# One FFN head's weights from two ScalarE passes, and its sums on VectorE in every other tile

## The chip, the cores and the metric

One core of a Trainium2 chip runs the program. The metric is the device time of one execution in microseconds (us), smaller being better; the median of three runs stands for the kernel.

## The reference

A pre-norm block over 16 sequences of 512 tokens with 128 channels: windowed attention with 16 heads, and then a feed-forward layer that picks its experts by product keys. Only the latter is touched by the change:

```python
xn = batchnorm(layernorm(x))                       # over all 8192 tokens
q = (xn @ w_q.T) -> 2 halves, 8 heads
sim = einsum(q, keys)                              # 32 similarities per half and head
sx, sy = top8(sim[0]), top8(sim[1])
scores, idx = top8 of the 64 sums sx[i] + sy[j]    # experts i * 32 + j, of 1024
o = gelu(x . key_in[idx]) * softmax(scores)
out = sum over heads and picked experts of o * key_out[idx]
```

## The kernel before

Attention runs first (to about 710 us) and is the same in both kernels. The FFN then works without a gather. For each tile of 128 tokens (64 tiles in 16 groups of 4, tile k = 0 to 3 of a group) and each of the 8 heads it makes a dense row of weights over all 1024 experts:

- GpSimd (`pair_sums`, L772) adds the 32 similarities of one half to the 32 of the other: SUM, 1024 elements per token, in a ring of 16 buffers, two tiles' worth. A buffer is free when the mask that reads it has run (`sum_buffer_free`).
- ScalarE (L873) makes E = exp(SUM + NB) into one of two PSUM buffers. NB = -log(sum) - maximum, so E is the softmax value. Exp h waits for the pair sum h and for mask h-2, whose E buffer it takes.
- VectorE (L965) makes W = (SUM >= the eighth best score) * E, the "mask". W has 8 buffers.
- TensorE (L1033) turns W with eight transposes per head and adds up the heads in PSUM (WT), in one buffer.
- After head 7 VectorE (`experts`, L948) multiplies WT by the Gelu values GE of all experts to CT, inside the next tile (h=1), and TensorE multiplies CT by key_out (`outputs`, L997 and L1000).

The order of each engine's work is written out by hand as a loop over the heads h of a tile. VectorE also does the ranking for the tiles ahead, in eight parts (`choose`): 0 to 3 are MAX8 over the similarities, 4 and 5 the candidates and the top 8 of each head (TOP), with D8 = scores less their maximum; 6 is the sum Z of their exps and 7 is NB. EVEN_PARTS and ODD_PARTS say ahead of which mask each part stands: in even tiles parts 0 to 5 of the next tile and 0, 1 of the one after stand ahead of mask 4, in odd tiles 2 and 3 ahead of masks 2 and 3, and 4, 5 ahead of mask 4; parts 6 and 7 ahead of masks 6 and 7 in both. ScalarE copies products out of PSUM between its exps (GE at h=1 and h=3, OUT at h=5, SIM at h=7), does a small exp and a logarithm for the next tile after exps 5 and 6, and in even tiles, behind exp 3, applies Gelu to half of a group's GE, between two table loads (L806, L807). M8X and TOP are in PSUM (SMALL), M8Y, CD, D8, Z, LZ, NB and SIM in SBUF.

L404 and L410 are two small operations of VectorE in attention. Both take two tensors of 32x128: L404 one from PSUM and one from SBUF, L410 (rm and mp) both from SBUF. GpSimd runs L261 in attention, the masking of the exps.

Of the kernel before, what the change touches and what calls it, by code (L numbers as in the profile page):

```python
# [33 lines left out]
P = 128  # L34
# [630 lines left out]
WRING = 8  # L665

EVEN_PARTS = ((), (), (), (), ((1, 0), (1, 1), (1, 2), (1, 3), (1, 4), (1, 5), (2, 0), (2, 1)), (), ((1, 6),), ((1, 7),))
# [7 lines left out]
def ffn(nc, ctx, x1, x2T, KM, key_in, key_out, gb, ident, bnst, first, out):  # L675
# [6 lines left out]
    def sem(name):  # L682
# [23 lines left out]
    NB = [sb(f"NB{b}", [P, FH]) for b in range(2)]  # L706
    SUM = [sb(f"SUM{b}", [P, NE]) for b in range(RING)]
# [6 lines left out]
    SMALL = ps("SMALL", [P, 4, FH, TOPK])  # L714
# [6 lines left out]
             "out_stored ranked candidates top_ready top_less_max top_exp exp_sum log_sum bias_ready").split()  # L721
# [46 lines left out]

    def pair_sums(eng, j, h, q):
# [4 lines left out]
    def sum_buffer_free(eng, j, h):  # L774

        wait_pos(eng, S["weights_masked"], j * FH + h - RING + 1)

    @block.gpsimd
    def _(pool):
# [5 lines left out]
        def group(g, b, more):  # L785
            for k in range(GT):
                j = g * GT + k
                pool.wait_ge(S["sim_copied"], j + 1)
                for h in range(FH):
                    sum_buffer_free(pool, j, h)  # L790
                    pair_sums(nc.gpsimd, j, h, k).then_inc(S["pair_sums"], 1)
# [4 lines left out]
    def _(act):  # L796
# [45 lines left out]

        small_exp(0)
        small_ln(0)

        def group(g, b, more):
            for k in range(GT):
# [4 lines left out]
                for h in range(FH):  # L852
# [18 lines left out]
                    act.wait_ge(S["pair_sums"], j * FH + h + 1)  # L871
                    wait_pos(act, S["weights_masked"], j * FH + h - 1)
                    nc.scalar.activation(E[h % 2][:, :], SUM[(k * FH + h) % RING][:, :], ACT.Exp, bias=NB[q][:, h:h + 1]).then_inc(S["exp_ready"], 1)  # L873

# [13 lines left out]
    def _(dve):  # L888
# [13 lines left out]
        def choose(part, j, r, q):  # L902
# [19 lines left out]
            if part == 5:  # L922
# [6 lines left out]
                nc.vector.tensor_tensor(D8[:, :, :], TOP[q][:, :, :], CD[:, :, 0:1].broadcast_to([P, FH, TOPK]), ALU.subtract).then_inc(S["top_less_max"], 1)  # L929
            if part == 6:  # L930
                dve.wait_ge(S["top_exp"], j + 1)
                nc.vector.tensor_reduce(Z[:, :], E8[:, :, :], AX.X, ALU.add).then_inc(S["exp_sum"], 1)
            if part == 7:
                dve.wait_ge(S["log_sum"], j + 1)

                nc.vector.scalar_tensor_tensor(out=NB[q][:, :], in0=LZ[:, :], scalar=-1.0, in1=TOP[q][:, :, 0], op0=ALU.mult, op1=ALU.subtract).then_inc(S["bias_ready"], 1)

# [12 lines left out]
        def group(g, b, more):  # L950
            for k in range(GT):
# [4 lines left out]
                for h in range(FH):  # L956
# [3 lines left out]
                    if h == 1 and real:  # L960
                        experts(*prev)

                    dve.wait_ge(S["exp_ready"], j * FH + h + 1)
                    wait_pos(dve, S["weights_turned"], j * FH + h - WRING + 1)
                    nc.vector.scalar_tensor_tensor(out=W[h % WRING][:, :], in0=SUM[(k * FH + h) % RING][:, :], scalar=TOP[q][:, h, TOPK - 1:TOPK],  # L965
                                                   in1=E[h % 2][:, :], op0=ALU.is_ge, op1=ALU.mult).then_inc(S["weights_masked"], 1)
# [5 lines left out]
    def _(pe):  # L972
# [30 lines left out]
        def group(g, b, more):  # L1003
            for k in range(GT):
                j = g * GT + k
                real = not (isinstance(j, int) and j == 0)
                for h in range(FH):
# [19 lines left out]
                    pe.wait_ge(S["weights_masked"], j * FH + h + 1)  # L1027
# [70 lines left out]
```

## Time and profile before

| | us |
|---|---|
| median of three runs | 1721.02 (1718.32 to 1722.32) |
| profiled execution | 1717.66, its span 1715.9 |
| busy: TensorE, VectorE, ScalarE, GpSimd | 1490.5, 1502.3, 1264.6, 1330.6 |
| GpSimd's pair sums, 512 of them | 958.5 |
| VectorE's masks, 512 | 641.9 |
| ScalarE's exps, 512 | 566.6 |
| TensorE's granted clock, mean | 0.956 of full speed |

The sums, masks and exps are all in the FFN, some 1000 us long. Four engines are busy for some 85 to 100% of it, so busy shares don't name the bound by themselves; the order of starts within a pair of tiles does, and the groups of rows below follow that order. A duration in the rows is that of one instruction as recorded; neighbours on one engine overlap by some 0.05 to 0.1 us, so the distance between two starts is a little less than the duration.

### The profile page before, as it was taken

The numbers are of one execution on the slowest core, as the hardware profiler recorded it, in microseconds if no ns is written. First come the engines' busy times: TensorE is split into PE (matmuls) and PEld (weight loads), VectorE is DVE, ScalarE is ACT, GpSimd is POOL, SyncE is SP. The second block draws the span as 40 slices with busy tenths as digits, with TensorE's granted clock in tenths as the row PEclk, the third lists the DMA queues.
The fourth block names the chain that finished last, engine by engine and source line by source line (L and its number), as shares of the span: only waits on it lengthen the run. The fifth ranks groups of instructions, "written<-read, shape, count | busy, mean of one in ns | idle before, by whom it ended". The sixth has DMA issues, their size and how long they took to land.

```text
span 1715.9 us, 33034 instructions
## 1 busy us (share of the span) xinstructions
PE 1490.5 (87%) x10688; PEld 1029.4 (60%) x10688; DVE 1502.3 (88%) x4488; ACT 1264.6 (74%) x1741; POOL 1330.6 (78%) x1579
## 2 busy tenths in 40 slices
PE   3799999999999998678888888888888888888877
PEld 2355555555555554367667666676666766667766
DVE  3889999999999985389999999999999999999998
ACT  1166666666666666378888888888888888888885
POOL 1055555556655556499999999999999999999993
PEclk9799999999999999789999999999999999999999
DMA  5344445444555440100000000000000000000000
GB/s 139 88 99 105 109 111 118 111 110 103 119 113 111 103 103 22 62 1 19 1 20 20 1 19 19 7 13 19 19 1 20 20 1 19 19 8 13 14 7 7
DMA packets 73627, 86.37 MB, mean 50 GB/s; under 512 B 9872, under 2 KB 63760, under 8 KB 68752
## 3 DMA queue, kind: packets, MB, share of 16 engines
q1 hardware_dynamic: 73456, 84.27, 20.7%
q8 instruction: 85, 1.39, 0.4%
q14 instruction: 86, 0.70, 0.2%
HBM read 58.30 MB, written 25.95 MB: 49 GB/s over the span
## 4 chain that ended last, share of the span: by engine, by line
POOL 47%; issue 5%; ACT 3%; DVE 2%; PE 1%; ACTq 0%; DVEq 0%; SPq 0%
POOL SUM L772 47%; ACT E L873 2%; DVE W L965 2%; ACT L807 1%; ACT GE L806 0%; PE WT L1033 0%; PE MB L1000 0%; PE E L988 0%; DVE CT L948 0%; DVE M8Y L909 0%; DVE SMALL L926 0%; ACT L806 0%; ACT SIM L800 0%; PE MB L975 0%; DVE SMALL L909 0%
## 5 line engine op out<-in xcount | busy, mean ns | idle before, releaser
L772 POOL TENSOR_TENSOR SUM<-SIM 128x1024 f32<-128x1024 f32 x512 | 958.5, 1928 | 11.5 <-DVE W L965 7.9
L965 DVE SCALAR_TENSOR_TENSOR W<-SUM,SMALL,E 128x1024 f32<-128x1024 f32 x512 | 641.9, 1279 | 46.4 <-ACT E L873 44.7
L873 ACT ACTIVATE E<-SUM,NB 128x1024 f32<-128x1024 f32 x512 | 566.6, 1118 | 102.1 <-DVE W L965 86.9
L1033 PEld LDWEIGHTS WT<-idf,W 128*128 128x128 f32 x4096 | 497.3, 151 | 231.3 <-DVE W L965 120.6
L1033 PE MATMUL WT<-idf,W 128*128 128x128 f32 x4096 | 570.8, 292 | 69.3 <-DVE CT L948 38.0
L261 POOL TENSOR_SCALAR_AFFINE_SELECT PT<-PT 128x128 f32<-128x128 f32 (+1 forms) x1024 | 336.9, 355 | 257.8 <-ACT PT L355 224.2
L414 DVE CUSTOM_DVE_ANT_0 SY<-SY,bandf 128x384 f32<-128x384 f32 x512 | 273.3, 574 | 0.0
L355 ACT ACTIVATE PT<-TX 128x512 f32<-128x512 f32 x256 | 153.0, 598 | 113.6 <-PE TX L542 113.4
L429 DVE TENSOR_REDUCE mx<-SX 128x2 f32<-128x512 f32 x256 | 174.5, 682 | 59.8 <-PE SX L524 59.7
L357 ACT ACTIVATE PT<-TY 128x768 f32<-128x768 f32 x256 | 207.4, 810 | 3.7
L570 PE MATMUL PV<-PT,V 128*32 128x384 f32 (+1 forms) x2048 | 165.5, 441 | 2.6 <-POOL PT L261 2.4
L516 PE MATMUL SY<-K,Q 72*128 72x384 bf16 x512 | 144.0, 339 | 8.4 <-DVE mx L414 4.3
L542 PE MATMUL TY<-Q,K 75*128 75x384 bf16 x512 | 125.9, 328 | 11.5 <-ACT PT L357 10.4
L975 PE MATMUL MB<-KM,BNT 128*128 128x512 f32 x128 | 72.1, 645 | 71.2 <-ACT OUT L820 69.4
L1000 PE MATMUL MB<-KO,CT 128*128 128x128 f32 x1024 | 124.9, 275 | 1.1 <-DVE CT L948 1.1
L516 PE MATMUL SX<-K,Q 72*128 72x256 bf16 x512 | 102.0, 281 | 24.4 <-DMA Q<-q_parts 18.9
L1000 PEld LDWEIGHTS MB<-KO,CT 128*128 128x128 f32 x1024 | 119.5, 192 | 1.3 <-DVE CT L948 1.3
L542 PE MATMUL TX<-Q,K 75*128 75x256 bf16 x512 | 99.6, 276 | 3.9 <-ACT PT L355 2.7
L948 DVE TENSOR_TENSOR CT<-WT,GE 128x1024 f32<-128x1024 f32 x64 | 78.4, 1225 | 20.2 <-PE WT L1033 20.2
L542 PEld LDWEIGHTS TX<-Q,K 75*128 75x128 bf16 x512 | 37.6, 98 | 97.2 <-issue 82.2
L570 PEld LDWEIGHTS PV<-PT,V 128*32 128x32 f32 x2048 | 53.6, 109 | 68.1 <-issue 47.9
L516 PEld LDWEIGHTS SX<-K,Q 72*128 72x128 bf16 x512 | 48.7, 100 | 67.3 <-issue 18.6
(110 smaller groups left out, 1638.9 us busy)
## 6 DMA issues: line engine op xcount, KB each, us to landing
K<-k_parts SPq DMA_DIRECT2D x96, 192.0 KB
Q<-q_parts SPq DMA_DIRECT2D x288, 64.0 KB
q_parts<-qp SPq DMA_DIRECT2D x16, 384.0 KB, 2.4
k_parts<-kp SPq DMA_DIRECT2D x16, 384.0 KB, 2.4
xin<-in_x SPq DMA_DIRECT2D x16, 256.0 KB, 3.1
xres<-in_x SPq DMA_DIRECT2D x16, 256.0 KB, 9.5
x<-X SPq DMA_DIRECT2D x16, 256.0 KB, 2.2
x2T<-X2T SPq DMA_DIRECT2D x16, 256.0 KB, 2.1
```

What stands on the lines that cost most here:

```text
L261: return nc.gpsimd.affine_select(out=out, in_=out, compare_op=ALU.is_ge, fill=0.0, base=0, pattern=([[0, 2]] if pairs else []) + [[s, P]], ...
L357: nc.scalar.activation(pt[:, 512:1280].rearrange("p (j n) -> p j n", j=2), TY[:, :, 0:384], ACT.Exp).then_inc(S["inner_exp"], 1)
L414: return nc.vector.tensor_tensor_reduce(out=scores, in0=scores, in1=bandf[:, k0 * P:k1 * P], scale=1.0, scalar=-3e38, op0=ALU.add, op1=ALU ...
L429: nc.vector.tensor_reduce(mx[:, h, 0:4:3], SX[:, :, :], AX.X, ALU.max).then_inc(S["outer_maxima"], 1)
L516: return pe.matmul(out, Q[b][0:KQ, h, i * P:(i + 1) * P], K[b][0:KQ, h, k0 * P:k1 * P], start=clear, stop=done, skip_group_check=True)
L542: return pe.matmul(out[:, 0:(q1 - q0) * P], K[b][0:R, h, j * P:(j + 1) * P], Q[b][0:R, h, q0 * P:q1 * P], start=True, stop=True, skip_grou ...
L570: o = pe.matmul(PV[32 * e:32 * e + 32, q0 * P:q1 * P], V[b][:, slot:slot + SLOT_V], PT[:, h % 8, at:at + (q1 - q0) * P], start=(j == 0 and ...
L772: return eng.tensor_tensor(SUM[(q * FH + h) % RING][:, :].rearrange("p (i j) -> p i j", i=NK), sx, sy, ALU.add)
L873: nc.scalar.activation(E[h % 2][:, :], SUM[(k * FH + h) % RING][:, :], ACT.Exp, bias=NB[q][:, h:h + 1]).then_inc(S["exp_ready"], 1)
L965: nc.vector.scalar_tensor_tensor(out=W[h % WRING][:, :], in0=SUM[(k * FH + h) % RING][:, :], scalar=TOP[q][:, h, TOPK - 1:TOPK], in1=E[h % ...
L1000: o = pe.matmul(po, CT[k % 2][:, e, :], key_out[:, e, :], start=False, stop=(e == BLK - 1))
L1033: o = pe.matmul(WT[:, e, :], W[h % WRING][:, e * P:(e + 1) * P], ident[:, :], is_transpose=True, start=(h == 0 and e % 4 == 0), stop=(h == ...
```

## The change

Head 3 (LH) gets its weights in another way, and in odd tiles its pair sum comes from another engine.

- ScalarE: ahead of exp 2 it applies Prelu in place to head 3's SUM with bias NT = -(eighth best score) and a slope of 1e30 for negative values (`l_shift`). A selected sum keeps its distance to the eighth best, another one becomes hugely negative. At h=3, in place of exp 3, a second pass writes exp(SUM + NL) straight to W[3] in SBUF (`l_exp`), with NL = (eighth best - maximum) - log(sum). What isn't selected comes out as 0.
- VectorE: no mask of head 3. It makes NT in part 5 and NL in part 7, ahead of NB, one element per partition each. NL's inputs are D8 and LZ, both in SBUF; NT's is TOP in PSUM.
- In odd tiles GpSimd leaves head 3 out. VectorE makes that sum one tile ahead, in the even tile ahead of mask 4: a copy of 32 similarities to PSUM (XL, part 8), and at the end of the ranking there the addition (part 9) with XL from PSUM and the other half from SBUF.
- The waits count 7 masks per tile; E's two buffers alternate over those seven heads. TensorE waits for `l_weights` at head 3.

```diff
--- before.py
+++ after.py
@@ -663,8 +663,11 @@
 CAND = 20
 RING = 16
 WRING = 8
-
-EVEN_PARTS = ((), (), (), (), ((1, 0), (1, 1), (1, 2), (1, 3), (1, 4), (1, 5), (2, 0), (2, 1)), (), ((1, 6),), ((1, 7),))
+LH = 3
+MASKED = FH - 1
+SUMS_AHEAD = (0, 2)
+
+EVEN_PARTS = ((), (), (), (), ((1, 0), (1, 1), (1, 2), (1, 3), (1, 4), (1, 5), (1, 8), (2, 0), (2, 1), (1, 9)), (), ((1, 6),), ((1, 7),))
 ODD_PARTS = ((), (), ((1, 2),), ((1, 3),), ((1, 4), (1, 5)), (), ((1, 6),), ((1, 7),))
 
 SIM0 = 2
@@ -704,6 +707,8 @@
     Z = sb("Z", [P, FH])
     LZ = sb("LZ", [P, FH])
     NB = [sb(f"NB{b}", [P, FH]) for b in range(2)]
+    NT = [sb(f"NT{b}", [P, 1]) for b in range(2)]
+    NL = [sb(f"NL{b}", [P, 1]) for b in range(2)]
     SUM = [sb(f"SUM{b}", [P, NE]) for b in range(RING)]
     W = [sb(f"W{b}", [P, NE]) for b in range(WRING)]
     CT = [sb(f"CT{b}", [P, BLK, P]) for b in range(2)]
@@ -711,14 +716,16 @@
     E = [ps(f"E{b}", [P, NE]) for b in range(2)]
     WT = ps("WT", [P, BLK, P])
     MB = ps("MB2", [P, GN])
-    SMALL = ps("SMALL", [P, 4, FH, TOPK])
+    SMALL = ps("SMALL", [P, 5, FH, TOPK])
+    XL = SMALL[:, 4, 0:NK // TOPK, :].rearrange("p a b -> p (a b)")
     M8X = [SMALL[:, b, :, :] for b in range(2)]
     TOP = [SMALL[:, 2 + b, :, :] for b in range(2)]
 
     names = ("waits_passed half_set bn_mean bn_variance bn_rstd bn_coef x1_loaded x2T_loaded bn_rows "
              "sim_product sim_copied pair_sums exp_ready weights_masked weights_turned "
              "experts_weighted out_product out_copied expert_product expert_copied gelu_ready "
-             "out_stored ranked candidates top_ready top_less_max top_exp exp_sum log_sum bias_ready").split()
+             "out_stored ranked candidates top_ready top_less_max top_exp exp_sum log_sum bias_ready "
+             "l_x_moved l_sums l_shifted l_weights").split()
     S = {n: sem("f_" + n) for n in names}
 
     def steps(eng, do):
@@ -766,6 +773,22 @@
         steps(sp, group)
         store(GROUPS - 1, 1)
 
+    def sum_by_vector(j):
+
+        return j > 0 and (j - 1) % GT in SUMS_AHEAD
+
+    def sums_by_vector(j):
+
+        return sum(sum_by_vector(i) for i in range(j + 1))
+
+    def sums_by_pool(j, h):
+
+        return j * FH + h + 1 - sums_by_vector(j if h >= LH else j - 1)
+
+    def masked(j, h):
+
+        return j * MASKED + (h if h >= LH else h + 1)
+
     def pair_sums(eng, j, h, q):
         sx = SIM[q][:, 0, h, :].unsqueeze(2).broadcast_to([P, NK, NK])
         sy = SIM[q][:, 1, h, :].unsqueeze(1).broadcast_to([P, NK, NK])
@@ -773,7 +796,10 @@
 
     def sum_buffer_free(eng, j, h):
 
-        wait_pos(eng, S["weights_masked"], j * FH + h - RING + 1)
+        if h == LH:
+            wait_pos(eng, S["l_weights"], j - 1)
+        else:
+            wait_pos(eng, S["weights_masked"], masked(j - 2, h))
 
     @block.gpsimd
     def _(pool):
@@ -787,6 +813,8 @@
                 j = g * GT + k
                 pool.wait_ge(S["sim_copied"], j + 1)
                 for h in range(FH):
+                    if h == LH and sum_by_vector(j):
+                        continue
                     sum_buffer_free(pool, j, h)
                     pair_sums(nc.gpsimd, j, h, k).then_inc(S["pair_sums"], 1)
 
@@ -839,6 +867,21 @@
         def small_ln(j):
             act.wait_ge(S["exp_sum"], j + 1)
             nc.scalar.activation(LZ[:, :], Z[:, :], ACT.Ln).then_inc(S["log_sum"], 1)
+
+        def l_shift(j, k, q):
+
+            if sum_by_vector(j):
+                act.wait_ge(S["l_sums"], sums_by_vector(j))
+            else:
+                act.wait_ge(S["pair_sums"], sums_by_pool(j, LH))
+            s = SUM[(k * FH + LH) % RING][:, :]
+            nc.scalar.activation(s, s, ACT.Prelu, bias=NT[q][:, :], alpha=1e30).then_inc(S["l_shifted"], 1)
+
+        def l_exp(j, k, q):
+
+            act.wait_ge(S["l_shifted"], j + 1)
+            wait_pos(act, S["weights_turned"], (j - 1) * FH + LH + 1)
+            nc.scalar.activation(W[LH][:, :], SUM[(k * FH + LH) % RING][:, :], ACT.Exp, bias=NL[q][:, :]).then_inc(S["l_weights"], 1)
 
         small_exp(0)
         small_ln(0)
@@ -868,9 +911,15 @@
                         finish(j - 1, *((g, b, k - 1) if k else (g - 1, 1 - b, GT - 1)))
                     if h == COPY_SIM and (more or k < 1):
                         sim_copy(j + 3, (k + 3) % 4)
-                    act.wait_ge(S["pair_sums"], j * FH + h + 1)
-                    wait_pos(act, S["weights_masked"], j * FH + h - 1)
-                    nc.scalar.activation(E[h % 2][:, :], SUM[(k * FH + h) % RING][:, :], ACT.Exp, bias=NB[q][:, h:h + 1]).then_inc(S["exp_ready"], 1)
+                    if h == LH - 1:
+                        l_shift(j, k, q)
+                    if h == LH:
+                        l_exp(j, k, q)
+                    else:
+                        n = masked(j, h)
+                        act.wait_ge(S["pair_sums"], sums_by_pool(j, h))
+                        wait_pos(act, S["weights_masked"], n - 2)
+                        nc.scalar.activation(E[(n - 1) % 2][:, :], SUM[(k * FH + h) % RING][:, :], ACT.Exp, bias=NB[q][:, h:h + 1]).then_inc(S["exp_ready"], 1)
 
                     if h == 5 and nxt:
                         small_exp(j + 1)
@@ -927,13 +976,25 @@
                 o.then_inc(S["top_ready"], 1)
                 dve.wait_ge(S["top_ready"], j + 1)
                 nc.vector.tensor_tensor(D8[:, :, :], TOP[q][:, :, :], CD[:, :, 0:1].broadcast_to([P, FH, TOPK]), ALU.subtract).then_inc(S["top_less_max"], 1)
+                nc.vector.tensor_scalar(NT[q][:, :], TOP[q][:, LH, TOPK - 1:TOPK], -1.0, None, ALU.mult)
             if part == 6:
                 dve.wait_ge(S["top_exp"], j + 1)
                 nc.vector.tensor_reduce(Z[:, :], E8[:, :, :], AX.X, ALU.add).then_inc(S["exp_sum"], 1)
             if part == 7:
                 dve.wait_ge(S["log_sum"], j + 1)
-
+                nc.vector.tensor_tensor(NL[q][:, :], D8[:, LH, TOPK - 1:TOPK], LZ[:, LH:LH + 1], ALU.subtract)
                 nc.vector.scalar_tensor_tensor(out=NB[q][:, :], in0=LZ[:, :], scalar=-1.0, in1=TOP[q][:, :, 0], op0=ALU.mult, op1=ALU.subtract).then_inc(S["bias_ready"], 1)
+
+            if part == 8 and sum_by_vector(j):
+
+                nc.vector.tensor_copy(XL, SIM[r][:, 0, LH, :]).then_inc(S["l_x_moved"], 1)
+            if part == 9 and sum_by_vector(j):
+
+                dve.wait_ge(S["l_x_moved"], sums_by_vector(j))
+                wait_pos(dve, S["l_weights"], j - 1)
+                nc.vector.tensor_tensor(SUM[(r * FH + LH) % RING][:, :].rearrange("p (i j) -> p i j", i=NK),
+                                        XL.unsqueeze(2).broadcast_to([P, NK, NK]),
+                                        SIM[r][:, 1, LH, :].unsqueeze(1).broadcast_to([P, NK, NK]), ALU.add).then_inc(S["l_sums"], 1)
 
         dve.wait_ge(S["x2T_loaded"], 16)
         nc.vector.tensor_scalar(BNT[0][:, :], X2T[0][:, :], ab[:, 0:1], ab[:, 1:2], ALU.mult, ALU.add).then_inc(S["bn_rows"], 1)
@@ -960,10 +1021,13 @@
                     if h == 1 and real:
                         experts(*prev)
 
-                    dve.wait_ge(S["exp_ready"], j * FH + h + 1)
+                    if h == LH:
+                        continue
+                    n = masked(j, h)
+                    dve.wait_ge(S["exp_ready"], n)
                     wait_pos(dve, S["weights_turned"], j * FH + h - WRING + 1)
                     nc.vector.scalar_tensor_tensor(out=W[h % WRING][:, :], in0=SUM[(k * FH + h) % RING][:, :], scalar=TOP[q][:, h, TOPK - 1:TOPK],
-                                                   in1=E[h % 2][:, :], op0=ALU.is_ge, op1=ALU.mult).then_inc(S["weights_masked"], 1)
+                                                   in1=E[(n - 1) % 2][:, :], op0=ALU.is_ge, op1=ALU.mult).then_inc(S["weights_masked"], 1)
 
         steps(dve, group)
         experts(GROUPS * GT - 1, GROUPS - 1, 1, GT - 1)
@@ -1024,7 +1088,10 @@
                     if h == SLOT_B and more:
                         pe.wait_ge(S["sim_copied"], j + 4)
                         o_block(1 - b, 2 * k + 1)
-                    pe.wait_ge(S["weights_masked"], j * FH + h + 1)
+                    if h == LH:
+                        pe.wait_ge(S["l_weights"], j + 1)
+                    else:
+                        pe.wait_ge(S["weights_masked"], masked(j, h))
 
                     if h == 0:
                         wait_pos(pe, S["experts_weighted"], j)
```

## Rows read from the trace of the kernel before

**Rows 1.** The head of the page.
```profile
span 1715.9 us, 33034 instructions
```

**Rows 2.** Groups by line, 800 to 1700 us: count, busy us, mean ns, idle before.
```profile
L772 POOL TENSOR_TENSOR SUM<-SIM 128x1024 f32<-128x1024 f32 x470 | 880.0, 1930 | 8.0 <-DVE W L965 7.9
L965 DVE SCALAR_TENSOR_TENSOR W<-SUM,SMALL,E 128x1024 f32<-128x1024 f32 x470 | 589.3, 1279 | 41.5 <-ACT E L873 40.0
...
L873 ACT ACTIVATE E<-SUM,NB 128x1024 f32<-128x1024 f32 x471 | 521.3, 1118 | 91.3 <-DVE W L965 76.6 <-POOL SUM L772 11.7
...
L806 ACT ACTIVATE GE<-GE 128x2048 f32<-128x2048 f32 x29 | 55.5, 1915 | 0.3
...
L807 ACT ACT_TABLE_LOAD x29 | 37.2, 1283 | 0.5
```

**Rows 3.** GpSimd in order of time from 1362 us: start, us, what, idle before.
```profile
1387.98 29.98 POOL L772 TENSOR_TENSOR SUM<-SIM 128x1024 f32<-128x1024 f32 x16 [0.70 <-DVE W L965]
1418.67 7.53 POOL L772 TENSOR_TENSOR SUM<-SIM 128x1024 f32<-128x1024 f32 x4 [0.70 <-DVE W L965]
```

**Rows 4.** Windows of 100 us: length, PE, PEld, DVE, ACT, POOL busy (count), clock, DMA.
```profile
1200.00:1300.00 100.00, 85.05 (x550) 67.39 (x549) 91.39 (x263) 86.05 (x104) 100.00 (x54) 0.93 0.05 16
1300.00:1400.00 100.00, 87.04 (x586) 69.71 (x585) 92.11 (x258) 85.02 (x103) 98.57 (x54) 0.95 0.03 10
```

**Rows 5.** VectorE in order of time, an even, an odd and an even tile.
```profile
1386.62 2.49 DVE L965 SCALAR_TENSOR_TENSOR W<-SUM,SMALL,E 128x1024 f32<-128x1024 f32 x2 [0.41 <-ACT E L873]
...
1394.09 1.23 DVE L948 TENSOR_TENSOR CT<-WT,GE 128x1024 f32<-128x1024 f32 x1 [0.59 <-PE WT L1033]
...
1401.14 2.47 DVE L965 SCALAR_TENSOR_TENSOR W<-SUM,SMALL,E 128x1024 f32<-128x1024 f32 x2
...
1404.87 0.16 DVE L936 SCALAR_TENSOR_TENSOR NB<-LZ,SMALL 128x8 f32<-128x8 f32 x1
1405.52 2.48 DVE L965 SCALAR_TENSOR_TENSOR W<-SUM,SMALL,E 128x1024 f32<-128x1024 f32 x2 [0.49 <-ACT E L873]
1407.99 1.23 DVE L948 TENSOR_TENSOR CT<-WT,GE 128x1024 f32<-128x1024 f32 x1
1409.13 3.81 DVE L965 SCALAR_TENSOR_TENSOR W<-SUM,SMALL,E 128x1024 f32<-128x1024 f32 x3
1412.85 0.85 DVE L909 MAX8 SMALL<-SIM 128x8 f32<-128x32 f32 x8
...
1417.30 2.49 DVE L965 SCALAR_TENSOR_TENSOR W<-SUM,SMALL,E 128x1024 f32<-128x1024 f32 x2 [0.40 <-ACT E L873]
```

**Rows 6.** ScalarE in order of time, same stretch.
```profile
1396.60 1.12 ACT L873 ACTIVATE E<-SUM,NB 128x1024 f32<-128x1024 f32 x1 [1.06 <-DVE W L965]
...
1404.36 2.16 ACT L873 ACTIVATE E<-SUM,NB 128x1024 f32<-128x1024 f32 x2
...
1406.93 2.28 ACT L873 ACTIVATE E<-SUM,NB 128x1024 f32<-128x1024 f32 x2
...
1410.50 1.12 ACT L873 ACTIVATE E<-SUM,NB 128x1024 f32<-128x1024 f32 x1 [0.67 <-POOL SUM L772]
...
1416.15 1.12 ACT L873 ACTIVATE E<-SUM,NB 128x1024 f32<-128x1024 f32 x1
```

**Rows 7.** TensorE in order of time, heads 4, 5 and 6, 7 of an even tile.
```profile
1388.07 3.37 PE L1033 MATMUL WT<-idf,W 128*128 128x128 f32 x16
...
1392.14 1.91 PE L1033 MATMUL WT<-idf,W 128*128 128x128 f32 x16
```

**Rows 8.** Two lines in attention: duration ns min/median/max, starts, forms.
```profile
L410 DVE TENSOR_TENSOR mp<-rm,mp x32: 274/354/510, 67.1 to 667.0; 32x128 bf16<-32x128 f32 x32
...
L404 DVE SCALAR_TENSOR_TENSOR rm<-MB,mp x32: 274/274/278, 63.7 to 664.7; 32x128 f32<-32x128 f32 x32
```

**Rows 9.** In order of time around 455 us, one L410 and GpSimd.
```profile
455.08 0.30 POOL L261 TENSOR_SCALAR_AFFINE_SELECT PT<-PT 128x128 f32<-128x128 f32 x1
...
455.15 0.36 DVE L410 TENSOR_TENSOR mp<-rm,mp 32x128 bf16<-32x128 f32 x1
```

## The prediction, made before the changed kernel was run

> **What bounds the kernel now.** I read the page first. Its 40 slices split the run into attention and, from about 710 us, the FFN; every edited line is in the FFN, so 1000 us are at stake. The page's chain of waits ascribes most of the FFN to GpSimd's sums, and the groups by line seem to agree: a sum is 1.93 us as recorded [rows 2]. But the count in that same view says otherwise. 470 masks in 900 us are 58.75 tiles, so a tile takes 15.32 us, and GpSimd's 16 sums in 29.98 us [rows 3] are 1.87 us each, 14.97 us a tile. GpSimd is the faster one: it is busy without a break in the 100 us windows up to 1300 us and falls short of that first in the next one [rows 4], when all 16 SUM buffers are full; from there it stops 0.70 us once in two tiles for a mask [rows 3]. The tile rate doesn't change at that point, so GpSimd is not the bound. The sums matter only as a floor, at 14.97.
>
> The bound is VectorE and ScalarE passing the two E buffers between them, and it repeats every two tiles. VectorE's head-4 masks start at 1386.62 (an even tile), 1401.14 (odd) and 1417.30 (even) [rows 5]: 14.52 us from even to odd, 16.16 us from odd to even, 30.68 us a pair, 32 pairs. The long half is ScalarE's. From exp 7 at 1404.36 to exp 4 at 1416.15 it has one real gap, 0.67 us ahead of exp 3 at 1410.50. The row names GpSimd's sum, which was done long before; the other wait of exp 3 is for mask 1, and that one ends at 1409.13 + 1.28 = 1410.41 [rows 2, 5]. Then come table load, Gelu, table load [rows 6]. VectorE ranks meanwhile and still waits 0.4 us for exp 4. The short half is VectorE's: ScalarE idles 1.06 us at once ahead of exp 3 there [rows 6], and for shorter spans elsewhere. TensorE is third; it makes VectorE wait 0.59 us for WT in the even tile only [rows 5], since its heads 4 and 5 took 3.37 us there against 1.91 us for the 16 matmuls of heads 6 and 7 [rows 7].
>
> **The odd tile's half.** VectorE loses the mask of head 3. Three masks take 1409.13 to 1412.85, so one is worth 1.24 us. It gains NT, one element per partition. The nearest rows are NB, 0.16 us as recorded for 8 elements, and the eight MAX8 that follow each other in 0.85 us, 0.10 us apart [rows 5]; NT lies ahead of mask 4, on the path; I take 0.10, and nothing (if it slips into the wait for exp 4) to 0.16 as its ends. ScalarE gains a pass (1.04 us, below) in the half where one of its waits alone is as long. PE has the head's transposes to do as before. 14.52 - 1.24 + 0.10 = 13.38 us.
>
> **The even tile's half.** Here the sum for the next tile is added to VectorE: a PSUM and an SBUF input of 1024, like the 1.14 us from CT to the next mask (1407.99 to 1409.13); with XL and NT at 0.10 each that is 1.34 us, less the mask's 1.24. So VectorE ends 0.10 us later and its 0.4 us of waiting for exp 4 covers it. Without that cover each 0.1 us costs 3 us in the run. ScalarE: at h=2 the Prelu is put ahead of exp 2, and exp 3 gives way to the second pass. Prelu has no row. Gelu with double the elements, also from SBUF to SBUF, is 1915 ns and bounds it above; half of that bounds it below; exp over the same 1024 elements, 1118 ns as recorded [rows 2] and 1.04 us from start to start (two in 2.16 us [rows 6]), is nearest and is taken. Exp 1 starts at 1406.93 [rows 6]; Prelu 1407.97; exp 2 1409.02 (mask 0 is over by then); GE copy 1410.07; second pass 1410.55; table load 1411.71 instead of 1411.63. The new pass fills just the gaps of 0.67 and of exp 2, since neither it nor the second pass waits for a mask. 16.16 + 0.08 = 16.24 us. No pair sum is late: GpSimd is 5 to 15 heads ahead.
>
> GpSimd loses one sum in two tiles: 15 x 1.87 = 28.07 us a pair, which only lowers the floor. It is needed all the same, since 14.97 a tile would be above what follows. The DMAs, PE's order and the number of E, W and SUM buffers stay.
>
> So far a pair takes 13.38 + 16.24 = 29.62 us, 1.06 less, 34 us over 32 pairs.
>
> **The operation that spoils it.** NL = D8 - LZ has one element per partition, yet both its inputs are in SBUF, and GpSimd is in a sum nearly always. No operation of VectorE in the FFN loop has that now: M8X, TOP, E and WT are in PSUM. Attention has one, L410. It takes 274 ns alone, as L404 of its shape with a PSUM input always does, but 354 in the median and up to 510 [rows 8]. The one at 455.15 shows why: a select on GpSimd ran from 455.08 to 455.38, and L410 ended at 455.51, 0.13 us behind it [rows 9]. It waited for the instruction's end, and no further one of the queued selects got in ahead of it. A sum is six times as long as such a select. *The Trainium skill, SBUF — State Buffer, section Who interferes with whom, says that a VectorE instruction with two SBUF inputs contends with a GpSimd instruction that reads SBUF and that the later one blocks fully; the trace agrees, by these ends. The page by itself would give 0 to 1.93 us per NL, and it speaks against the change.*
>
> What it costs depends on where in a sum NL falls. NL stands where NB is now, 3.73 us after mask 4 starts (1401.14 to 1404.87); mask 7 starts at 4.38, because it waits 0.65 us for exp 7 [rows 5]. Once the ring is full, GpSimd restarts 1.37 us after mask 4 starts (1417.30 to 1418.67) [rows 3, 5], in both tiles of a pair now, as its seven sums (13.1 us) and eight sums (15.0 us) are shorter than the halves. NL then meets the second sum, which ends at 1.37 + 2 x 1.87 + 0.06 (a sum is recorded so much longer than its distance to the next) = 5.17. NB follows, and mask 7 starts at about 5.30, 0.92 us late. In the odd tile exp 1 has only 0.13 us of slack to mask 7 (1405.52 + 1.28 against 1406.93 [rows 5, 6]), and ScalarE's full chain hangs on it: 0.8 us go through. In the even tile TensorE's 0.59 us hides much: masks 7 and 0 end at 1394.09 - 0.59 = 1393.50 now, mask 7 so at 1392.30; it will end at 1393.22, head 7's eight transposes (half of 1.91, and 0.1 for handing over) follow, and CT starts at about 1394.36 instead of 1394.09 [rows 5, 7]: 0.3 us. A pair is 29.62 + 0.8 + 0.3 = 30.72 us, against 30.68 now. The whole gain is given back.
>
> Until the ring is full GpSimd runs freely and NL adapts to the ends of sums: a pair is then the next whole number of sums above 29.62, which is 16 x 1.87 = 29.94, a gain of 0.74. Now GpSimd gains 15.34 - 14.97 = 0.37 us a tile on the masks and needs 39 tiles to fill the ring, so there is 14.5 us of room; with 29.94 - 28.07 = 1.87 us a pair it is full after 8 pairs. Sum: 8 x -0.74 + 24 x 0.04 = -5 us. From the profiled execution's 1717.66 (span 1715.9 and 1.8 around it) [rows 1] that is 1712.7; the median of the three runs is 1721.02, 3.4 higher, so 1716. Its own bounds: a delay 0.15 us smaller or larger in each tile is 2 x 24 x 0.15 = 7 us, and NT's ends are 1 to 2 us: 1707 to 1727.
>
> **Rivals.** (1) *NL doesn't wait.* One element may slip in between, or its wait lies in the 0.65 us before mask 7. Then the 1.06 us a pair stay: 1721 - 34 = 1687. For it: the recorded rule is from 128 elements a partition and from selects, not from sums. Against it: L410 waited each time a select was running. (2) *NL waits less than I make of it.* GpSimd's phase falls so that NL meets the end of a sum in one of the tiles: 29.62 + 0.3 = 29.92, near 16 sums, all the way: 24 us less, 1697. (3) *Slower: the wait is paid in both tiles.* If PE's heads 4 and 5 aren't slow any more, or the sum on VectorE is 0.3 us longer than CT and the even half loses its cover, then both delays of 0.92 go through: 29.62 + 1.84 = 31.46, 0.78 above now, 25 us: 1746. It decides from the point where less than 0.3 us of the 0.59 is left. If a queued sum got in ahead of NL each time, it would be 1.87 more a tile, but L410's row speaks against that. (4) *The new function brings table loads,* two of 1.28 us a tile [rows 2], over 100 us. Every load in the trace stands at a Gelu, and copies and Identity run between the exps without one. *The Trainium skill, ScalarE: Activation LUTs, section Table sets: the hidden batching unit, says that cheap functions are in every set; it doesn't name Prelu.* (5) *The change does nothing*, because VectorE's head 3 is hidden anyway: against it, VectorE is what the odd half waits for. That would be 1721.
>
> **Chances.** My case 0.50, rival 1 0.17, rival 2 0.13, rival 3 0.14, rival 4 0.02, rival 5 0.04. About 0.2% (3.4 us) is what a measurement can tell from no change. My case, 1707 to 1727 around 1716, is faster by that in 0.26, within it in 0.17, slower in 0.07. With the rivals: faster 0.56, same 0.21, slower 0.23. The range goes from 1688, close to rival 1, to 1742.
>
> **What would show it.** NL's rows: 0.16 us each if free, about 1.5 us and an end at a sum's end if not. VectorE's 0.65 us of idle time ahead of mask 7 would go too. The distance of even to odd head-4 masks: 13.4 if free, 13.7 late in the run; odd to even 16.2 if free, 17.0 if not. GpSimd should begin to pause near 970 us and pause twice a pair. Prelu and second pass at 1.1 us each; table loads at the Gelus alone. I am wrong if the pair is 29.6 throughout (NL), or above 31 (cover), or if the odd half doesn't shrink at all (PE or ScalarE).

## The result, and the profile after

The changed kernel is slower: 1744.06 us in the median of four runs (1743.06 to 1746.79), against 1719.67 us for the kernel before next to it. The ratio is 1.0149, with a 95% interval of 1.012 to 1.0178. The profiled execution's span is 1742.3 us, 26.4 more than before [rows 1]. 1716 was forecast, so the prediction was wrong by 28 us, and the time lies above its range, which ended at 1742.

From the page of the changed kernel, its head and some of its costliest lines (line, engine, what, count, busy us, mean ns, idle time before it and its releaser):

```profile
span 1742.3 us, 33161 instructions
...
L795 POOL TENSOR_TENSOR SUM<-SIM 128x1024 f32<-128x1024 f32 x480 | 900.9, 1914 | 94.1 <-DVE W L1029 90.8
...
L1029 DVE SCALAR_TENSOR_TENSOR W<-SUM,SMALL,E 128x1024 f32<-128x1024 f32 x448 | 567.0, 1280 | 28.3 <-ACT E L922 28.2
L922 ACT ACTIVATE E<-SUM,NB 128x1024 f32<-128x1024 f32 x448 | 499.7, 1116 | 91.2 <-DVE NB L986 72.6
...
L985 DVE TENSOR_TENSOR NL<-D,LZ 128x1 f32<-128x1 f32 x64 | 103.4, 1616 | 0.3 <-ACT LZ L869 0.3
```

The sums fell to 480, the masks to 448, as intended. New on the page is NL, an operation on one element per partition: 64 of them cost VectorE 103.4 us, 1616 ns on average. GpSimd, hardly ever idle before [rows 2], now waits 90.8 us for masks. The new instructions between 800 and 1700 us (groups by line, same columns):

```profile
L985 DVE TENSOR_TENSOR NL<-D,LZ 128x1 f32<-128x1 f32 x58 | 82.9, 1430 | 0.0
...
L884 ACT ACTIVATE W<-SUM,NL 128x1024 f32<-128x1024 f32 x58 | 66.6, 1148 | 0.0
L878 ACT ACTIVATE SUM<-SUM,NT 128x1024 f32<-128x1024 f32 x58 | 66.0, 1137 | 0.0
...
L995 DVE TENSOR_TENSOR SUM<-SMALL,SIM 128x1024 f32<-128x1024 f32 x29 | 35.0, 1206 | 0.0
...
L979 DVE TENSOR_SCALAR NT<-SMALL 128x1 f32<-128x1 f32 x57 | 8.4, 148 | 0.0
```

The two passes, the sum on VectorE and NT cost about what was forecast (1148, 1137, 1206 and 148 ns). NL is far above the 150 ns of NT, which has as many elements.

How it looks late in the run, an even, an odd and an even tile. VectorE in order of time (start, us, what, idle before it):

```profile
1376.91 2.50 DVE L1029 SCALAR_TENSOR_TENSOR W<-SUM,SMALL,E 128x1024 f32<-128x1024 f32 x2 [0.70 <-ACT E L922]
...
1384.54 1.22 DVE L1009 TENSOR_TENSOR CT<-WT,GE 128x1024 f32<-128x1024 f32 x1
...
1387.64 1.28 DVE L1029 SCALAR_TENSOR_TENSOR W<-SUM,SMALL,E 128x1024 f32<-128x1024 f32 x1 [0.31 <-ACT E L922]
...
1391.00 2.47 DVE L1029 SCALAR_TENSOR_TENSOR W<-SUM,SMALL,E 128x1024 f32<-128x1024 f32 x2
...
1394.73 1.43 DVE L985 TENSOR_TENSOR NL<-D,LZ 128x1 f32<-128x1 f32 x1
1396.08 0.15 DVE L986 SCALAR_TENSOR_TENSOR NB<-LZ,SMALL 128x8 f32<-128x8 f32 x1
1396.15 2.55 DVE L1029 SCALAR_TENSOR_TENSOR W<-SUM,SMALL,E 128x1024 f32<-128x1024 f32 x2
...
1408.24 2.49 DVE L1029 SCALAR_TENSOR_TENSOR W<-SUM,SMALL,E 128x1024 f32<-128x1024 f32 x2 [0.69 <-ACT E L922]
```

ScalarE in the same stretch (BNT, a pass over a group's input, made once in four tiles; then exp 7; exp 0 of the next tile; exp 1; table load; exp 4):

```profile
1384.76 0.80 ACT L843 ACTIVATE BNT<-X2T,ab 128x512 f32<-128x512 f32 x1
...
1394.22 1.12 ACT L922 ACTIVATE E<-SUM,NB 128x1024 f32<-128x1024 f32 x1
1396.26 1.12 ACT L922 ACTIVATE E<-SUM,NB 128x1024 f32<-128x1024 f32 x1 [0.93 <-DVE NB L986]
...
1397.80 1.12 ACT L922 ACTIVATE E<-SUM,NB 128x1024 f32<-128x1024 f32 x1
...
1402.57 1.28 ACT L834 ACT_TABLE_LOAD   x1
...
1407.09 1.12 ACT L922 ACTIVATE E<-SUM,NB 128x1024 f32<-128x1024 f32 x1
```

and GpSimd:

```profile
1378.27 13.15 POOL L795 TENSOR_TENSOR SUM<-SIM 128x1024 f32<-128x1024 f32 x7 [2.23 <-DVE W L1029]
1392.35 15.01 POOL L795 TENSOR_TENSOR SUM<-SIM 128x1024 f32<-128x1024 f32 x8 [0.94 <-DVE W L1029]
1409.60 13.14 POOL L795 TENSOR_TENSOR SUM<-SIM 128x1024 f32<-128x1024 f32 x7 [2.24 <-DVE W L1029]
```

The odd tile's mask 4 starts at 1391.00. GpSimd restarts at 1392.35. NL starts at 1394.73 and ends at 1396.16, as GpSimd's second sum ends (1392.35 + 1.87 + 1.91 = 1396.13). NB can't start before, and exp 0 of the next tile, which waits for NB's bias, stands idle for 0.93 us. The waits by total time say the same for 900 us:

```profile
ACT E L922 <- DVE NB L986: 53.2, 58, 0.9
```

That is once in each of the 58 tiles. From exp 7 to exp 1 ScalarE now takes 3.58 us (1394.22 to 1397.80), 2.57 before (1404.36 to 1406.93 [rows 6]), and since it is busy without a gap from there to exp 4, all of it goes through: odd to even is 17.24 us (1391.00 to 1408.24), against 16.16 [rows 5]. Even to odd is 14.09 us in this pair (1376.91 to 1391.00), where ScalarE makes BNT, and 13.68 in the next, where it doesn't; the two alternate through the run. A pair is so 31.13 us on average, 0.4 to 0.45 above the 30.68 to 30.74 of most pairs before, and 30 pairs make some 13 us. That is half of the loss.

The other half is one single wait. VectorE (with the last NL of the run too), GpSimd and ScalarE near the start of the FFN:

```profile
744.64 0.42 DVE L985 TENSOR_TENSOR NL<-D,LZ 128x1 f32<-128x1 f32 x1
...
757.72 15.37 DVE L985 TENSOR_TENSOR NL<-D,LZ 128x1 f32<-128x1 f32 x1
773.02 0.15 DVE L986 SCALAR_TENSOR_TENSOR NB<-LZ,SMALL 128x8 f32<-128x8 f32 x1
...
1721.20 0.15 DVE L985 TENSOR_TENSOR NL<-D,LZ 128x1 f32<-128x1 f32 x1
```

```profile
718.86 54.22 POOL L795 TENSOR_TENSOR SUM<-SIM 128x1024 f32<-128x1024 f32 x29 [3.23 <-ACT SIM L828]
774.45 3.78 POOL L795 TENSOR_TENSOR SUM<-SIM 128x1024 f32<-128x1024 f32 x2 [1.37 <-DVE W L1029]
```

```profile
773.21 1.12 ACT L922 ACTIVATE E<-SUM,NB 128x1024 f32<-128x1024 f32 x1 [14.87 <-DVE NB L986]
```

The third NL takes 15.37 us. GpSimd doesn't pause in its first 29 sums, and NL ends at 773.09 with the last of them. The 30th, head 7 of tile 3, needs the buffer that the mask of head 7 in tile 1 frees, and that mask stands behind NL: GpSimd goes as far as the ring lets it while VectorE stands still. ScalarE stands idle for 14.87 us. The first pair of tiles takes 44.55 us between head-4 masks, where it took 30.82 before. 13.7 + 13 us are the loss of 26.4, nearly. The last NL, at 1721.20, takes 0.15 us: GpSimd's last sum ended at 1710.59.

### The profile page after: what moved, and what is told of

The parts are those of the page before. It is cut to its first block, busy times and chain, and to the rows that moved or that the text cites. A ratio compares the mean times of both kernels' runs of the same rounds, so it can differ in the third digit from the quotient of the medians.

```text
span 1742.3 us, 33161 instructions
## 1 busy us (share of the span) xinstructions
PE 1468.5 (84%) x10688; PEld 1008.1 (58%) x10688; DVE 1565.0 (90%) x4616; ACT 1318.5 (76%) x1805; POOL 1273.1 (73%) x1547
## 4 chain that ended last, share of the span: by engine, by line
ACT 17%; DVE 14%; POOL 11%; issue 10%; PE 5%; DMA 1%; DVEq 0%; SPq 0%; ACTq 0%
POOL SUM L795 11%; ACT E L922 8%; DVE W L1029 8%; PE WT L1100 3%; ACT L835 2%; ACT L834 2%; ACT W L884 2%; DVE SMALL L975 1%; DVE M8Y L958 1%; DVE NL L985 1%; ACT SUM L878 1%; PE MB L1039 1%; ACT GE L834 1%; ACT BNT L843 1%; PE E L1052 0%
## 5 line engine op out<-in xcount | busy, mean ns | idle before, releaser
L795 POOL TENSOR_TENSOR SUM<-SIM 128x1024 f32<-128x1024 f32 x480 | 900.9, 1914 | 94.1 <-DVE W L1029 90.8
L1100 PE MATMUL WT<-idf,W 128*128 128x128 f32 x4096 | 545.7, 283 | 109.4 <-DVE W L1029 67.3
L1100 PEld LDWEIGHTS WT<-idf,W 128*128 128x128 f32 x4096 | 475.1, 146 | 267.5 <-DVE W L1029 144.3
L1029 DVE SCALAR_TENSOR_TENSOR W<-SUM,SMALL,E 128x1024 f32<-128x1024 f32 x448 | 567.0, 1280 | 28.3 <-ACT E L922 28.2
L922 ACT ACTIVATE E<-SUM,NB 128x1024 f32<-128x1024 f32 x448 | 499.7, 1116 | 91.2 <-DVE NB L986 72.6
L985 DVE TENSOR_TENSOR NL<-D,LZ 128x1 f32<-128x1 f32 x64 | 103.4, 1616 | 0.3 <-ACT LZ L869 0.3
```

The source lines that it names most:

```text
L795: return eng.tensor_tensor(SUM[(q * FH + h) % RING][:, :].rearrange("p (i j) -> p i j", i=NK), sx, sy, ALU.add)
L922: nc.scalar.activation(E[(n - 1) % 2][:, :], SUM[(k * FH + h) % RING][:, :], ACT.Exp, bias=NB[q][:, h:h + 1]).then_inc(S["exp_ready"], 1)
L1100: o = pe.matmul(WT[:, e, :], W[h % WRING][:, e * P:(e + 1) * P], ident[:, :], is_transpose=True, start=(h == 0 and e % 4 == 0), stop=(h == ...
```

## The experiments

Two theories stood at the start. A: NL waits for GpSimd's running sum because both its tensors come from SBUF, and what stands behind it pays. B: the two passes load ScalarE too much (C, in e2b: any further operation in that place costs this). A third one, F, is about the long wait: it comes while GpSimd still runs freely. Each ratio is to runs of the kernel before made beside it, with medians of 1719.67 us (changed kernel), 1716.45 (e1, e2, e2b, e3) and 1720.24 (e1b, e5, e6); e7 and e8 were run once, and serve for their traces.

| run | us, median | ratio to before, 95% |
|---|---|---|
| changed kernel | 1744.06 | 1.012 to 1.0178 |
| e1: NL from PSUM | 1684.36 | 0.9781 to 0.9835 |
| e1b: NL from SBUF, LZ as a scalar | 1685.75 | 0.979 to 0.9842 |
| e2: kernel before + NL | 1776.89 | 1.0317 to 1.0379 |
| e2b: kernel before + NL from PSUM | 1717.09 | 0.9983 to 1.0013 |
| e3: NL behind NB | 1730.92 | 1.0049 to 1.011 |
| e5: e1 with all sums on GpSimd | 1689.84 | 0.9824 to 0.9864 |
| e6: GpSimd held close | 1712.5 | 0.995 to 0.9982 |
| e7: waits on the first sums | 1748.39 | one run |
| e8: operation ahead of mask 2 | 1788.45 | one run |

**e1, NL without a second tensor from SBUF.**

```diff
-nc.vector.tensor_tensor(NL[q][:, :], D8[:, LH, TOPK - 1:TOPK], LZ[:, LH:LH + 1], ALU.subtract)
+nc.vector.tensor_scalar(NL[q][:, :], TOP[q][:, LH, TOPK - 1:TOPK], TOP[q][:, LH, 0:1], LZ[:, LH:LH + 1],
+                        ALU.subtract, ALU.subtract)
```

> The changed kernel, with NL made by one instruction of the same size that takes its tensor input from PSUM (TOP, with the maximum and LZ as per-partition scalars) instead of two tensors in SBUF. Theory A (NL waits for GpSimd's running sum, and NB, the mask of head 7 and exp 0 stand behind it): NL falls from 1.43 to about 0.16 us, the single wait of 15.4 us at 758 us is gone, GpSimd runs freely for longer, a pair of tiles takes about 29.7 us instead of 31.1, and the time is 1685 to 1695. Rival B (the two passes on ScalarE are too much for it whatever NL does): a pair stays above 30.7 and the time at 1725 or more.

1684.36 us, just below the expected 1685 to 1695 and 60 us less than the changed kernel, with one instruction replaced by another of the same size. Groups by line, 800 to 1700 us:

```profile
L922 ACT ACTIVATE E<-SUM,NB 128x1024 f32<-128x1024 f32 x414 | 458.0, 1116 | 16.4 <-DVE W L1029 13.7 <-DVE NB L986 0.6 <-POOL SUM L795 0.6
...
L985 DVE TENSOR_SCALAR NL<-SMALL,LZ 128x1 f32<-128x1 f32 x59 | 16.3, 276 | 0.0
```

NL takes 0.28 us, and exps hardly wait for NB any more (0.6 us in place of 53.2). VectorE, at the head-4 masks and one NL:

```profile
1330.38 2.49 DVE L1029 SCALAR_TENSOR_TENSOR W<-SUM,SMALL,E 128x1024 f32<-128x1024 f32 x2 [0.53 <-ACT E L922]
...
1343.88 2.47 DVE L1029 SCALAR_TENSOR_TENSOR W<-SUM,SMALL,E 128x1024 f32<-128x1024 f32 x2
...
1347.61 0.28 DVE L985 TENSOR_SCALAR NL<-SMALL,LZ 128x1 f32<-128x1 f32 x1
...
1360.11 2.49 DVE L1029 SCALAR_TENSOR_TENSOR W<-SUM,SMALL,E 128x1024 f32<-128x1024 f32 x2 [0.54 <-ACT E L922]
...
1367.65 1.23 DVE L1009 TENSOR_TENSOR CT<-WT,GE 128x1024 f32<-128x1024 f32 x1 [0.66 <-PE WT L1100]
```

Even to odd 13.50 us, odd to even 16.23 us; over pairs 3 to 28 a pair is 29.65 us on average, with 29.62 forecast for the case that NL is free. GpSimd first pauses at 1020 us, 970 forecast. A holds, B falls: the passes cost ScalarE nothing that it didn't have. This is also the version that beats both kernels.

The halves from even to odd tiles vary from 12.92 to 13.91 us and average 13.4. What tells them apart is TensorE's granted clock while it turns the weights of heads 4 and 5 (columns as in [rows 4], the clock third from the end):

```profile
1302.50:1304.70 2.20, 2.08 (x17) 1.78 (x17) 2.20 (x4) 2.01 (x5) 2.11 (x2) 1.00 0.03 7
1361.50:1364.50 3.00, 3.00 (x16) 3.00 (x16) 2.69 (x5) 2.84 (x5) 3.00 (x2) 0.50 0.01 3
```

In 8 of those 26 pairs the clock is at 2.4 GHz there, the 16 matmuls take 2.30 us, CT doesn't wait for WT, and the half is 12.92 to 13.13 us. In the other 18 it falls to 1.2 GHz for 3.4 us around them, CT waits for WT (0.66 us at 1367.65), and the half is 13.41 to 13.91. TensorE had waited 2.4 us for ScalarE's copy of OUT ahead of either row. In the kernel before, the clock is at 1.2 GHz there in all 26, and CT waits for WT in each (0.59 us at 1394.09 [rows 5]).

**e1b, the same values in SBUF, but LZ as a per-partition scalar.**

```diff
-nc.vector.tensor_tensor(NL[q][:, :], D8[:, LH, TOPK - 1:TOPK], LZ[:, LH:LH + 1], ALU.subtract)
+nc.vector.tensor_scalar(NL[q][:, :], D8[:, LH, TOPK - 1:TOPK], LZ[:, LH:LH + 1], None, ALU.subtract)
```

> The changed kernel with the same two values in SBUF for NL, but LZ given as a per-partition scalar instead of a second tensor. Theory A in its narrow form (two tensors from SBUF make it wait): no wait, NL 0.16 to 0.3 us, 1682 to 1690. Rival H (any small operation that reads only SBUF waits for GpSimd here): NL 1.4 us and 1744.

```profile
L985 DVE TENSOR_SCALAR NL<-D,LZ 128x1 f32<-128x1 f32 x59 | 12.2, 208 | 0.0
```

0.21 us and 1685.75 us. Reading SBUF alone doesn't make it wait; with two tensors from SBUF it does.

**e2 and e2b, NL alone in the kernel before, and its control.**

```diff
+nc.vector.tensor_tensor(NX[:, :], D8[:, 3, TOPK - 1:TOPK], LZ[:, 3:4], ALU.subtract)          # e2
+nc.vector.tensor_tensor(NX[:, :], TOP[q][:, 3, TOPK - 1:TOPK], LZ[:, 3:4], ALU.subtract)      # e2b
 nc.vector.scalar_tensor_tensor(out=NB[q][:, :], in0=LZ[:, :], scalar=-1.0, ...)
```

> The kernel before, with nothing but the subtraction of two one-element SBUF tensors put ahead of NB (its result isn't used). Theory A: each waits some 1.4 us for a sum; the half from odd to even tiles grows by 1.0 us, the other by 0.3 to 0.5, so 1.3 to 1.5 us a pair and 42 to 48 us in all, 1762 to 1768, and some 14 more if a single long wait shows up. Rival B (the wait mostly lies in the 0.65 us before the mask of head 7): at most 0.3 us a pair, 1730 or less.

> The control to the run before: the same additional subtraction, but with its first input from PSUM. Theory A: 0.16 us long each, hidden in the 0.65 us before the mask of head 7, 1719 to 1722. Theory C (any additional instruction of VectorE there costs, not the port): as the other one, above 1740.

e2 is 60 us slower than the kernel before, e2b is not to be told from it. In e2 a pair is 31.92 us against 30.73, 1.2 more where 1.3 to 1.5 was expected: odd to even grows by 1.07 (17.23), as expected, even to odd by only 0.1 (14.67). The long wait is there too (VectorE in order of time):

```profile
759.04 18.50 DVE L937 TENSOR_TENSOR NX<-D,LZ 128x1 f32<-128x1 f32 x1
777.46 0.15 DVE L938 SCALAR_TENSOR_TENSOR NB<-LZ,SMALL 128x8 f32<-128x8 f32 x1
```

In e2b the groups by line show:

```profile
L937 DVE TENSOR_TENSOR NX<-SMALL,LZ 128x1 f32<-128x1 f32 x59 | 8.9, 150 | 0.0
```

150 ns with one input from PSUM. So the price belongs to the two SBUF tensors, not to the place, and it isn't bound to the rest of the change. e2's long wait ends with sum 31 (15 masks are done, 15 + 16 = 31). The next sum is head 7 of tile 3 there too; the two sums more are GpSimd's, as it makes all of them.

**e3, NL behind NB.**

```diff
-NL[q] = D8 - LZ                       # ahead of NB
 NB[q] = ...  .then_inc(bias_ready)
+NL[q] = D8 - LZ  .then_inc(nl_ready)  # and l_exp waits for nl_ready
```

> The changed kernel with NL issued behind NB instead of ahead of it; NL waits as before, but exp 0 of the next tile, which waits for NB, doesn't. Theory D (0.2 us of each delay in the half from odd to even tiles, and all of the lateness of ScalarE in tiles with BNT, comes from NB standing behind NL): exp 0 no longer waits, a pair takes 30.8 instead of 31.1 us, 8 to 12 us less than the changed kernel, 1732 to 1736. Rival E (the mask of head 7 alone carries the delay): no change, 1744.

1730.92 us, 13 less than the changed kernel and a little below the expected 1732 to 1736. NL waits as before (1.36 us), but ScalarE's exp 0 follows exp 7 at once, and the wait moves to exp 1, shorter (ScalarE in order of time):

```profile
1385.99 2.16 ACT L923 ACTIVATE E<-SUM,NB 128x1024 f32<-128x1024 f32 x2
...
1389.23 1.12 ACT L923 ACTIVATE E<-SUM,NB 128x1024 f32<-128x1024 f32 x1 [0.56 <-DVE W L1030]
```

Over pairs 3 to 28 a pair is 30.62 us on average (13.71 and 16.91), 0.53 less than the changed kernel's 31.15 over the same pairs. So D holds, and NB behind NL was worth 0.53 us a pair. With NL behind NB a pair is what the prediction had worked out for NL ahead of it, 30.72, within 0.1 us. The long wait, 15.65 us at 759.53, is there as before.

**e5, how much the sums on VectorE are worth.**

```diff
 def sum_by_vector(j):
-    return j > 0 and (j - 1) % GT in SUMS_AHEAD
+    return False                       # on top of e1
```

> The kernel of the first run (NL with its tensor input from PSUM), but GpSimd makes all the pair sums, VectorE none (no copy to XL, no addition, 512 sums on GpSimd). Theory A: a pair of tiles can't be shorter than GpSimd's 16 sums of 1.87 us, 29.94 us, against 29.64 measured in the first run: some 0.3 x 31 = 9 us slower than that, 1690 to 1697, and GpSimd never pauses. Rival G (the half in which ScalarE is full sets the time, and the sums on VectorE are of no use): as the first run, 1682 to 1687.

```profile
1200.00:1300.00 100.00, 87.11 (x596) 69.04 (x595) 89.24 (x259) 93.85 (x114) 100.00 (x54) 0.97 0.05 17
```

In this window of 100 us (columns as in [rows 4]) GpSimd is busy throughout, and so in all others; a pair is 29.87 us on average, close to its 16 sums (29.94). The intervals of e1 and e5 overlap (those of e1b, which ran beside e5, too), so the difference of some 4 to 5 us rests on the pairs more than on the medians. Nearly all of the gain is head 3's missing mask; the sums on VectorE add 0.2 us a pair.

**e6, GpSimd held close.**

```diff
-wait_pos(eng, S["l_weights"], j - 1)            # head 3
+wait_pos(eng, S["l_weights"], j)
-wait_pos(eng, S["weights_masked"], masked(j - 2, h))
+wait_pos(eng, S["weights_masked"], masked(j - 1, h))
```

> The changed kernel with GpSimd allowed only one tile ahead of the masks instead of two (each sum waits for the mask of the same head one tile before). NL still waits in each tile. Theory F (the single wait of 15.4 us comes because GpSimd still runs freely at that time, with its waits for masks passed long before, and lets NL in only when it pauses): GpSimd is tied to the masks from 735 us on, no NL is longer than 1.9 us, and the time is 13 to 15 us less than the changed kernel's, 1729 to 1732, with a pair still at 31.1 us. Rival I (the long wait belongs to the start of the FFN, whatever GpSimd does): a wait of 15 us is still there, 1744.

All NLs of this run (count: shortest, median, longest in ns):

```profile
L985 DVE TENSOR_TENSOR NL<-D,LZ x64: 393/1424/1960, 731.8 to 1688.7; 128x1 f32<-128x1 f32 x64
```

No wait is over 1.96 us, so the long one is gone, as F has it and I doesn't. But the time, 1712.5, is 31 us less than the changed kernel's instead of 14: I had expected a pair of 31.1, and it is 30.35. GpSimd's place against NL has shifted: the NLs made in even tiles are still 1.43 us, those made in odd tiles 0.44 and 0.86 in turn, and the halves from odd to even 16.25 and 16.66 us. What an NL costs depends on where in a sum of GpSimd's it starts.

**e7, waits that have passed ahead of the first sums.**

```diff
+eng.wait_ge(S["sim_copied"], 1)        # shortened: for tiles 0 and 1, which had no wait
```

> The changed kernel with a wait on a semaphore that has passed already ahead of each of the first 16 sums, which have none so far (all later ones have). In the changed kernel the first two NLs fall into these 16 sums and end with the sum that runs or the next one; the third, among sums with passed waits, is held for eight sums. Theory J (a sum with a passed wait of its own is what gets in ahead of NL): now the first NL, at 728 us, is held until the ring is full and GpSimd pauses, at about 719 + 16 x 1.87 = 749 us, 20 us. Rival K (only that GpSimd is free matters, and the first two got in by chance of their place): the first NL is 1.7 us as before and the third is long.

VectorE in order of time, the first two NLs:

```profile
731.34 1.77 DVE L985 TENSOR_TENSOR NL<-D,LZ 128x1 f32<-128x1 f32 x1 [0.28 <-ACT LZ L869]
...
747.66 15.32 DVE L985 TENSOR_TENSOR NL<-D,LZ 128x1 f32<-128x1 f32 x1
```

Neither J nor K. The first NL isn't held (1.77 us), but the second is (15.32 us), which was 0.42 us in the changed kernel, at the same place against the running sum (1.5 us after its start in both) and with nothing else changed. A passed wait on the sums that follow seems to matter, but it isn't all. The time, 1748.39 us, is one run.

**e8, another place.**

```diff
 if h == 2:
+    nc.vector.tensor_tensor(NX[:, :], gb[:, 0:1], ab[:, 0:1], ALU.subtract)    # kernel before, ahead of mask 2
```

> The kernel before, with a subtraction of two one-element SBUF tensors put ahead of the mask of head 2 in each tile instead of ahead of NB (its result isn't used). There GpSimd is in the middle of a row of sums, the next of which wait for masks that ran before the current sum began. Theory L (a sum whose wait had passed when the one before it began comes ahead of the waiting operation; only one released later lets it in): in tiles late in the run waits of more than 1.9 us, up to GpSimd's next pause, which comes soon since the masks stop: 2 to 6 us each, and the run is far above 1740. Rival M (the operation always gets in at the end of the sum that runs, and the long wait at the start of the FFN has another cause): every wait after the first few is 1.9 us or less.

```profile
L964 DVE TENSOR_TENSOR NX<-GB,ab x64: 153/1586/15733, 737.4 to 1770.8; 128x1 f32<-128x1 f32 x64
```

One long wait again, the second of the run at 757 us (15.73 us), and all others at 1.71 us or less. The waits go M's way, and L's forecast of 2 to 6 us is wrong. It doesn't settle L itself, though: in all the later cases the next sum had been released after the running one began (0.4 us or more), because GpSimd follows the masks more closely there than I thought. e6 speaks against L: 15 of its NLs got in ahead of a sum whose mask had ended 0.2 us before the running sum began. The pair is 32.1 us in most of the run, which took 1788.45 us.

## Why the prediction was wrong, point by point

**What bounds the kernel.** Right. The pair of tiles, and not GpSimd, sets the time: e1 takes the wait away and a pair is 29.65 us, with 29.62 from the sum (13.38 and 16.24 forecast, 13.4 and 16.23 measured). The passes at exp's price and the cover for VectorE's sum (it ended and VectorE still waited 0.70 us for exp 4) held. The 13.38, though, was met in part by luck: it took over the 0.59 us of waiting for WT from the kernel before, and e1's halves are 12.9 to 13.1 us or 13.4 to 13.9 with TensorE's clock. Table loads are 63 in both kernels, so rival 4 is out (one of them, at 11 us in attention, doesn't stand at a Gelu, which the prediction says of all).

**NL waits for the running sum.** Right, and in size: 1.43 us each, with its end at the sum's end, GpSimd restarting after mask 4 in both tiles of a pair. Mask 7 starts 5.15 us after mask 4, 5.30 forecast. Rival 1, on which 0.17 stood, isn't what this instruction does; e1, with another one, shows the time that it gave (1684, 1687 forecast).

**What the wait costs.** Here the first step failed. I let mask 7 alone carry the delay. NB stands between the two, and the prediction names it, but asks only when mask 7 can start, not who waits for NB. Exp 0 waits for NB's bias; so ScalarE loses 1.0 us, not 0.8, in the odd to even half. In every other pair ScalarE also makes BNT (0.80 us) ahead of exp 2, and its lateness reaches mask 2 in the even to odd half (0.31 us of idle time ahead of it at 1387.64; 14.09 us in place of 13.68). 31.13 us a pair instead of 30.72 is 12 us over 30 pairs. e3 puts NB ahead and finds 30.62. There the odd to even half is 0.67 us above 16.24, near what mask 7 alone gives with its measured delay: 5.15 - 4.38 = 0.77, less 0.13 of slack.

**The time before the ring is full.** This was the larger failure. I forecast eight pairs at 29.94 us, a gain of 6 us, from GpSimd's free run. In fact the long wait falls into this free run: 15.4 us once, at 758 us, and the ring is full right then, so that no pair at 29.94 comes behind it. From -6 to +14 is 20 us. With the 12 above that makes 32; the profiled execution, forecast at 1712.7, took 31.3 more. I had written that a queued sum getting in ahead of NL "would be 1.87 more a tile" and put it aside, since L410 had shown the opposite; its selects come in rows of two or four of 0.3 to 0.4 us each, where NL has up to 16 sums before it. It is e2, e3, e7 and e8 that show the wait to come back in other kernels, once in each, and e6 that it doesn't come when GpSimd is tied to the masks. In all five kernels that have it, it ends where the next sum needs the very buffer that the first mask behind the waiting operation frees.

**The cover by TensorE** in the even tile gave the forecast number: VectorE doesn't wait for WT any more (CT at 1384.54 follows mask 0 without a gap), and in pairs without BNT the half is 13.68 as forecast. It is so at either clock of TensorE, which is at 2.4 GHz there in 12 of the pairs 3 to 28: VectorE comes later than WT either way, and 13.68 is e1's 12.92 at full clock and 0.77 of delay. Rival 3 gave nearly the right time (1746) from the wrong mechanism. Its condition, that heads 4 and 5 aren't slow any more, came true in those 12 pairs, but it put the delay of 0.92 on top of 13.38, which still holds a wait for WT that goes with the slow heads. Two small slips in the range, of 1 to 2 us, change nothing: NT at nothing is worth 3 us and not 2, and 7 + 2 above 1716 is 1725.

**What stays open.** Why the long wait catches the second or third operation and not the first. The state in which it happens: GpSimd runs freely and the sums that follow have waits that passed long ago (for the next sum, its mask had ended 11.5 us before the running sum began in the changed kernel, 13.7 in e2, 15.6 in e8). In the 60 later tiles of the changed kernel that mask ended 0.58 us after the running sum had begun: GpSimd had to wait for it itself. That would fit a rule by which only a sum that is free early enough gets in ahead; but sums without waits let NL in (changed kernel, first and second), so did the first NL of e7, with passed waits, and so did the 15 sums of e6 that were free 0.2 us before the running one began. No run here tells which condition is the deciding one.

## What to carry to other kernels

Before a small VectorE instruction is put beside a busy GpSimd, look where its tensors lie: with two of them in SBUF an operation on one element took 1.4 us here, and putting one in PSUM or making it a per-partition scalar turned a kernel that was 1.5% slower into one that is 1.9% faster. Price such a wait by every instruction queued behind it, the one-element ones first, and follow who waits for each. And don't take an engine that runs freely ahead to be harmless: here it was only while GpSimd had free buffers that it kept VectorE out for 15 us, and the mask that would have stopped it stood behind the waiting operation.

## What the runs showed of the hardware

- A VectorE instruction with two tensors in SBUF waited for the end of GpSimd's running sum (once, in e3, for the end of the next one; it had come 0.07 us before the running one ended), and ended 0.01 to 0.02 us after it (1.43 us in most tiles of the changed kernel), though it has one element per partition. With GpSimd's sums over it took 0.15 us (1721.20), with one tensor from PSUM 0.15 us (e2b), with one SBUF tensor and a scalar from SBUF 0.21 us (e1b), and with one PSUM tensor and two scalars 0.28 us (e1).
- Usually it got in ahead of the next sum, which in 60 tiles of the changed kernel had become free 0.58 us after the running one began. Once per run it didn't, for eight or nine sums beyond the running one: 15.4 us in the changed kernel, 18.5 in e2, 15.7 in e3 and e8, 15.3 in e7. It never happened in e6.
- Prelu from SBUF to SBUF with a bias per partition took 1137 ns for 1024 elements, 21 more than exp to PSUM in the same run, and brought no table load (63 before and after); exp to SBUF instead of PSUM took 1148 ns against 1116.
- TensorE's granted clock fell from 2.4 to 1.2 GHz for 3.4 us at heads 4 and 5 of the even tile, in all of pairs 3 to 28 of the kernel before and in 18 of those 26 in e1; 16 matmuls of these heads took 2.30 us at the upper level and 3.55 at 1361.45 in e1, and the half of the pair was 12.9 to 13.1 us against 13.4 to 13.9.
